# A hand-written order of work: the last batch's values in its own step, the second queries and the first placing later in layer 1, the last projection two ticks later

## What is computed

```python
x = rotate(x)                                   # layer 0 of the reference
for layer in (1, 2, 3):                         # "layer 0, 1, 2" of the kernel's loops
    h = modulate(layernorm(x))
    q, k, v = split(h @ w_qkv + b_qkv)          # 16 heads of 18
    if layer == 2:
        q, k = ln(q) * g + b, ln(k) * g + b     # per head: the kernel's "tok", "root", "inverse"
    o = softmax(q @ k.T * scale) @ v
    x = x + gate * (o @ w_proj + b_proj)
    x = x + gate2 * mlp(modulate(layernorm(x))) # layer 3: top 2 of 4 experts
```

## Time and profile before

| what | value |
|---|---|
| median of 3 runs | 1814.21 us (1813.95 to 1819.57) |
| the profiled execution's own time | 1822.59 us |
| its span in the profile | 1820.8 us |
| PE matmul busy | 1643.5 us, 90% of the span |
| DVE busy | 1227.4 us, 67% |
| ACT busy | 1055.5 us, 58% |
| POOL busy | 674.1 us, 37% |
| mean granted clock of PE | 0.947 of full speed |
| attention part of layers 0, 1, 2 (first to last exponential) | 213.3 to 479.2, 662.6 to 967.0, 1130.4 to 1388.4 us |

### The profile page before, as it was taken

How to read it: one execution, slowest core, us unless ns; L and a number is a source line. 1 busy time by engine, 2 the same in 40 slices (tenths; PEclk the granted TensorE clock), 3 DMA queues, 4 the chain that set the end, 5 groups by cost and what they waited for, 6 DMA issues and landing times.

```text
span 1820.8 us, 28323 instructions
## 1 busy us (share of the span) xinstructions
PE 1643.5 (90%) x9431; PEld 1068.6 (59%) x9431; DVE 1227.4 (67%) x2685; ACT 1055.5 (58%) x1897; POOL 674.1 (37%) x661
## 2 busy tenths in 40 slices
PE   5876899998899897999899999999988989999997
PEld 2433444443488663444336976444435878999997
DVE  7872677775265576767733656777763776888885
ACT  2322476756546346776674533767667556777773
POOL 4431222213356332433244533223233373343442
PEclk9996799998899888999989999999999999999999
DMA  7721333223000222232310021333322445566662
GB/s 245 245 92 43 94 109 106 90 89 89 28 4 1 81 68 90 70 98 68 118 50 21 1 92 50 103 107 90 95 87 73 123 137 165 162 169 174 171 172 46
DMA packets 106768, 178.16 MB, mean 98 GB/s; under 512 B 14331, under 2 KB 61107, under 8 KB 106335
## 3 DMA queue, kind: packets, MB, share of 16 engines
q1 hardware_dynamic: 100336, 167.07, 30.1%
q0 software_dynamic: 6288, 9.29, 2.7%
HBM read 124.73 MB, written 51.09 MB: 97 GB/s over the span
## 4 chain that ended last, share of the span: by engine, by line
PE 62%; DVE 11%; ACT 9%; DMA 6%; issue 5%; POOL 3%; SPq 3%; ACTq 0%; DVEq 0%; POOLq 0%
PE ps L2184 21%; PE ps L2269 12%; PE ps L2237 8%; PE ps L2223 7%; PE ps L2347 6%; PE ps L2205 4%; DMA heads_t<-stage 3%; ACT Pr L2018 3%; PE ps L2323 1%; DMA raw<-in_w 1%; DVE negmax L1412 1%; DVE GT L1338 1%; PE ps L2074 1%; ACT HQ L1993 1%; SPq L924 1%
## 5 line engine op out<-in xcount | busy, mean ns | idle before, releaser
L1412 DVE TENSOR_REDUCE negmax<-ps 128x1 f32<-128x512 f32 x768 | 488.1, 680 | 219.7 <-PE ps L2205 215.8
L2018 ACT ACTIVATE Pr<-ps 128x512 f32<-128x512 f32 x768 | 410.9, 602 | 212.1 <-PE ps L2223 211.9
L2223 PE MATMUL ps<-QK 55*128 55x512 f32 x768 | 238.4, 512 | 37.3 <-ACT Pr L2018 25.8
L2269 PE MATMUL ps<-W2a,G 128*128 128x288 f32 x1512 | 230.7, 300 | 9.6 <-DVE G L1775 5.7
L2269 PEld LDWEIGHTS ps<-W2a,G 128*128 128x128 f32 x1512 | 213.8, 190 | 21.4 <-DVE G L1775 13.1
L2237 PE MATMUL ps<-Pr,V 128*32 128x512 f32 x1536 | 220.4, 648 | 0.0
L2205 PE MATMUL ps<-QK 54*128 54x512 f32 x768 | 194.8, 439 | 21.2 <-DMA QK<-HQ 7.8
L2223 PEld LDWEIGHTS ps<-QK 55*128 55x128 f32 x768 | 91.9, 190 | 201.1 <-ACT Pr L2018 107.9
L2184 PE MATMUL ps<-HQ,W1a 128*128 128x512 f32 (+3 forms) x756 | 182.0, 381 | 7.3 <-ACT g L2034 5.9
L1775 DVE TENSOR_TENSOR G<-g,G 128x512 fp32r<-128x512 f32 (+1 forms) x201 | 152.4, 763 | 40.7 <-ACT G L2045 36.4
L1169 POOL TENSOR_TENSOR HQ<-act,HQ 128x512 fp32r<-128x512 f32 (+3 forms) x72 | 93.0, 1292 | 190.2 <-ACT HQ L1993 134.2
(11 more groups left out here) (294 smaller groups left out, 2670.2 us busy)
## 6 DMA issues: line engine op xcount, KB each, us to landing
QK<-heads_t SPq DMA_DIRECT2D x192, 144.0 KB
heads_t<-stage SPq DMA_DIRECT2D x96, 252.0 KB
raw<-in_w SPq DMA_DIRECT2D x34, 576.0 KB
raw<-in_w SPq DMA_DIRECT2D x38, 432.0 KB
QK<-heads_t SPq DMA_DIRECT2D x192, 72.0 KB
tok_rows<-blank SPq DMA_DIRECT2D x4, 2700.0 KB, 20.8
XG<-tok_rows SPq DMA_DIRECT2D x11, 540.0 KB, 4.8
WP<-in_w SPq DMA_DIRECT2D x39, 144.0 KB, 3.5
```

The source lines that it names most:

```text
L1412: dve.tensor_reduce(negmax[:, m % 2, h, t:t + 1], ps[:, row_bank(l, s, i), :], AX, ALU.max, negate=True).then_inc(a_free, 1)
L2018: act.activation(Pr[:, t % 2, 2 * half + pair, :], ps[:, (16 * s + u) % 3, :], ACT.Exp, scale=SCALE).then_inc(b_free, 1)
L2223: mm(ps[:, k % 3, :], QK[r:r + QROW + 1, g, 1, pair, 128 * t:128 * t + 128], QK[r:r + QROW + 1, g, 0, pair, :], start=True, stop=True).the ...
L2269: ins = mm(ps[:, t, 0:C], g_at(n)[:, x, 128 * t:128 * t + 128], W2[w_ % 2][:, w, ft, :], start=ft == 0 and p == 0, stop=ft == FT - 1 and p ...
```

## The change

Nothing is added to or taken from the work; only ticks change. In `attention_window`: for the last batch (window b = 2, y = 3) the four blocks of values go to ticks 25, 27, 28 and 30, in all layers; before they were at 1, 9, 17, 25 in layers 0 and 2, and at 4, 6, 15, 22 in layer 1. In layer 1, in every window, the first two projections go one tick later (10, 12 to 11, 13), the second block of queries one tick later (9 to 10), and the placing of group 0 from 11 to 13. In `leaving`, in all layers, the four projections of the last batch go from ticks 6, 8, 10, 12 of the dense part to 8, 10, 12, 14. The changed file's lines from 2000 on are 4 higher.

```diff
+VALUES = (25, 27, 28, 30)
...
-        turns = (10, 12, 18, 20) if l == 1 else (6, 10, 14, 18)
+        turns = (11, 13, 18, 20) if l == 1 else (6, 10, 14, 18)
...
-            out += [(t, "v", l, y, k) for k, t in enumerate((1, 9, 17, 25))]
+            out += [(t, "v", l, y, k) for k, t in enumerate((1, 9, 17, 25) if y < B - 1 else VALUES)]
...
-            out += [(t, "place", l, y, g) for g, t in enumerate((11, 16, 24, 32))]
+            out += [(t, "place", l, y, g) for g, t in enumerate((13, 16, 24, 32))]
...
-            out += [(t, "qk", l, y, j) for j, t in enumerate((7, 9, 14, 17, 27))]
-            out += [(t, "v", l, y, k) for k, t in enumerate((4, 6, 15, 22))]
+            out += [(t, "qk", l, y, j) for j, t in enumerate((7, 10, 14, 17, 27))]
+            out += [(t, "v", l, y, k) for k, t in enumerate((4, 6, 15, 22) if y < B - 1 else VALUES)]
...
-    out += [(6 + 2 * t, "proj", l, B - 1, t) for t in range(TT)] + [(15, "b2", l, 0, 0)]
+    out += [(8 + 2 * t, "proj", l, B - 1, t) for t in range(TT)] + [(15, "b2", l, 0, 0)]
```

## The result

| kernel | time | against the kernel before |
|---|---|---|
| before | 1814.1 us (4 runs) | |
| changed | 1839.6 us (4 runs, 1834.4 to 1846.7) | 1.0141, 95% interval 1.0112 to 1.0170 |
| changed, measured again | 1837.3 us (9 runs) | 1.0106, 1.0070 to 1.0141 |

The forecast was 1810.8 with a range to 1819.0. By the one comparison the change costs 25.6 us, by the other 19.3. The profiled execution of the changed kernel is its fastest in the first comparison (1834.4, span 1832.6), that of before is a long one for its kernel (1822.6), so the two traces differ by only 12 us. 4.7 us of what is missing lie in the opening, which has nothing of the change in it (208.6 us in after, 213.3 in before) and whose length differs from one execution to the next: 207.7 to 213.3 over the 18 traces of this study. So I compare lengths of steps, never absolute times.

What follows compares the result with a forecast made beforehand. The prediction took PE, busy 90% of the span, as the bound. Its terms, -6.0 + (0.75 + 1.7 + 1.15) - 3.5 + (1.8 + 1.8 - 1.1) = -3.4 us, took the median 1814.2 to 1810.8 us, range 1803.5 to 1819.0.

Steps and rivals of the forecast that it cites:

- What is moved out of such a step is gained: Layers 0 and 2, steps 8 to 10: chain stays on PE, so moved work is gained if it lands where PE waits.
- Part 1: Last batch's values, layers 0 and 2: three blocks leave steps 8 to 10, -3.0 us a layer, -6.0 in all.
- DVE or ACT sets 3.64: a block gives 1.0 us: Layers 0 and 2, steps 8 to 10: without its value block a pair of ticks falls from 4.64 to 3.64 us.
- rival A: Steps 12 and 13: filled gaps keep PE at 2.4 GHz, another -5.7 us, so 1805.1; chance 0.25.
- Rival C: Before step 12: maxima and load held by something like DRAM traffic, the -6.0 given back; +2.6, so 1816.8; chance 0.10.
- Part 2: Layer 1's second queries at tick 10, three windows: block leaves a stall's cover; +0.75, +1.7 and +1.15 us.
- Batch 2: Layer 1's third window: value block and its wait leave tick 15, but the placing's transfer has no slack; +1.15 us (0.5 to 1.9).
- Part 3: Last batch's values, layer 1: -2.0 from step 8, net -1.5 around the last query block and step 12; -3.5 us.
- 2.7 of clock: Layer 1, steps 12 and 13: of some 10 us at 1.2 GHz, 2.7 us come back if the gap no longer drops the clock.
- Part 4: Last projection, begin of the dense parts: +1.8 us each in layers 0 and 1, -1.1 in layer 2.
- in layer 2 the 1.98 us of waiting go: Begin of layer 2's dense part: PE's wait for oT vanishes, gates' product waits some 0.9 for DVE; -1.1 us.
- Rival B: Table loads and dense parts of layers 0 and 1: longer stalls lower the clock, +6.8 us in all, 1821.0; chance 0.10.

Runs made afterwards that it cites:

- h4: Kernel before with the last batch's second, third and fourth projection one tick earlier (6, 7, 9, 11) in layers 0 and 1: -1.5 us (-6.5 to +3.8).
- g4: Kernel before with, in layer 2 alone, the third and fourth block of the last projection two ticks later (6, 8, 12, 14): +3.1 us (-3.5 to +9.4).
- f4: Kernel before with only layer 1's first two projections at ticks 11 and 13 in place of 10 and 12: +5.4 us (0.4 to 10.5).
- g3: Kernel before with the last batch's values at 25, 27, 28, 30 in layers 0 and 2, at 15, 25, 28, 30 in layer 1: 0.0 us (-4.4 to +4.4).
- e4: Kernel before with only layer 1's second queries at tick 10, first two projections at 11 and 13, first placing at 13: +9.3 us (4.4 to 14.4).
- e1: Kernel before with only the last projection two ticks later in all three layers: +11.0 us (7.1 to 14.9).
- f1: The changed kernel itself, unaltered, measured again beside the kernel before: +19.3 us (12.7 to 25.6).
- h3: Changed kernel with the last projection as before, timed against the kernel before: +10.3 us (5.4 to 15.2).
- f3: Kernel before with the last projection two ticks later in layer 2 alone: +10.0 us (5.3 to 14.7).
- h2: Changed kernel with layer 1's second queries, projections and placing as before, timed against the kernel before: +14.9 us (8.9 to 20.9).
- e2: Kernel before with the last batch's values at ticks 25, 27, 28 and 30 in layers 0 and 2 alone: -0.7 us (-6.0 to +4.7).
- f2: Kernel before with the last projections two ticks later and layer 2's fourth weight load, third window, at tick 9 for 8: +15.1 us (7.8 to 22.3).
- g2: Kernel before with the last batch's values later in all layers and layer 2's fourth weight load, third window, at 10 for 8: +3.5 us (-2.4 to +9.4).

## Why the prediction was wrong, point by point

All 18 traces, sorted by whether the part is in. Means of a stretch's length in us, with the range; worked out from the starts of the exponentials that begin each step, a dense part from the start of the last one before it (h4 is left out of the first three rows, g4 of the fourth, f4 of the last; the row of layer 1's values leaves out g3 and every kernel with e4's or f4's lines).

```
stretch                          with the part            without                  difference
dense part, layer 0: leave        6: 186.2 (185.7-186.7)   11: 183.2 (182.4-184.0)   +3.0
dense part, layer 1: leave        6: 166.2 (165.9-167.4)   11: 164.6 (162.3-165.4)   +1.7
step 0, layer 2: leave in 0, 1    6:  18.3 (18.1-18.6)     11:  16.3 (14.9-19.8)     +2.0
dense part, layer 2: leave        6: 439.2 (436.6-442.9)   11: 434.0 (432.6-437.9)   +5.1
steps 8-15, layer 0: values       8: 131.2 (129.1-134.7)   10: 132.5 (128.6-138.1)   -1.2
steps 8-15, layer 2: values       8: 130.2 (128.1-134.1)   10: 130.2 (127.8-132.5)   -0.1
steps 8-15, layer 1: values       4: 142.2 (138.7-146.1)    8: 141.7 (139.0-144.4)   +0.5
steps 0-15, layer 1: queries      4: 309.5 (306.6-313.6)   13: 302.1 (298.4-308.1)   +7.4
```

The differences add to +18.4 us, beside +19.3 timed. The scatter of the traces allows some 6 us either way on that sum: the dense parts of layers 0 and 1 and layer 2's first step are certain to 1 us, the dense part of layer 2 to 2, and the rows of the steps to 2 to 4 each. The first four rows (+11.8) stand beside e1's +11.0, the last beside e4's +9.3. What no row has, the opening aside, takes 243.0 us in before, in after and in f1. So the result is placed in these rows, to that accuracy.

- **What bounds the kernel.** "What is moved out of such a step is gained" failed. The chain was on PE from score to score, but DVE was full in the same ticks, and ACT's exponentials held PE's scores too.
- **Part 1 (-6.0; found -1.3).** The failed step is the price of a block: "DVE or ACT sets 3.64: a block gives 1.0 us". The bare pair came from another layer's step without a half projection, and its length was taken as DVE's limit. In this pair DVE has six maxima, the transpose and the reciprocal, 4.5 us without a gap (rows of DVE above). The pair went from 4.64 to 4.66, the whole of steps 8 to 10 from 52.6 to 52.4. That is 0.2 us for three blocks, and the traces repeat to 0.1 us: even the lower bound, 0.6 a block, was too high. (The -1.2 of the table's longer stretch can't be told from 0.) That the blocks would fit into the 3.63 before step 12 was right (0.85 left); that SP's queue moves 3 us earlier was not, since nothing ahead of it had become shorter. Steps 12 to 15 are shorter by 0.2 and 0.3 in the mean, so rival A's prize for filling the gap did not come either. Rival C gave these -6.0 back as well, but by a queue held in DRAM; it was the gain that had never been there. The 2.6 us that the prediction quotes for a spill from the Trainium skill (page "DMA: Bandwidth & Descriptors", section "Anatomy of one DMA") is an estimate by a fit that the section gives for DMAs issued by POOL (GpSimd); this spill is SP's, took 5.14, and no term hangs on the 2.6.
- **Part 2 (+3.6; found +7.4).** Batch 0: forecast +0.75 (0 to 1.2), the traces -0.4, with up to 5 us between traces, so no more than small, as forecast: step 1 is 2.6 longer and step 2 2.7 shorter, for the placing's wait takes it back. Batch 1: forecast +1.7, the traces +1.4. Batch 2: forecast +1.15, steps 8 to 15 +6.7 (with 12 traces without it), and there the term fell. Step 9 is 3.6 longer in the three traces that have the last batch's values too than in the four with the values alone (24.4 against 20.8). The rest lies in steps 10 to 15, which differ by 3 us with the clock alone, whatever the edits (step 13: 18.2 us at 0.88 in before and in h3, 21.3 at 0.72 in after), so part of the 6.7, and of the 7.4, may be chance. Two things were missing in both windows that have a projection: that the first projection, now right behind the query block, waits for ACT to empty their bank (0.82 in step 5, 0.52 in step 9), and the clock, which in step 9 goes from 0.85 to 0.78. And where the value block left tick 15 its wait of 1.01 went, as the forecast had it, but another came in its place, for the exponentials (step 9 of after):

```profile
858.60 0.40 PE L2227 MATMUL ps<-QK 55*128 55x512 f32 x1
860.26 0.79 PE L2227 MATMUL ps<-QK 55*128 55x512 f32 x1 [1.26 <-ACT Pr L2022]
```

  The transfer that the forecast took for the bound of batch 2 shows no wait in after: PE comes too late for it to be one.
- **Part 3 (-3.5; found +0.5).** The wait behind the last query block was right to 0.05 us, and step 12's wait took most of it, as forecast. Steps 8 to 11 became 4.5 us longer and 12 to 15 were 4.0 shorter, where the forecast had 6.5 (3.8 of wait and 2.7 of clock). What failed are the -2.0 in step 8 (it gave 0.5: 18.9 for 19.4) and the 2.7 of clock "given back".
- **Part 4 (+2.5; found +11.8).** The mechanism in layers 0 and 1 was right, waits and block (+1.8 each; +3.0 and +1.7). The failed step is "in layer 2 the 1.98 us of waiting go": the forecast never asked what is late next. It was POOL's shift and what follows it, in whose shadow the wait lay. -1.1 became +4.5 at tile 8: 2.2 for the block, 1.7 for the wait of the gates' product, which the forecast had seen and priced at 0.9, and 1.4 for half clock after the 3.10 us wait (3.25 for the seven matmuls at 1413.09, 1.89 for the same seven at full speed), less the 0.8 by which that wait ends earlier. Of the 4.5 some is won back further on: f1 and f3, without the late scatter, are 2.8 and 3.1 late at tile 28, but h2 5.6. The 2.0 in layer 2's first step (granted clock 0.63 in 8 us of it, below) neither the forecast nor a rival had named.
- **Rival B** had the sign and, with +6.8, a third of the size. Its clock is part of it, not most: over the nine runs of f1 the mean granted clock is 0.952, over the 29 of before beside them 0.954, by which the changed kernel spends 0.002 x 2 x 1830 = some 7 us more at 1.2 GHz, worth at most 4 of its 19 us. The Trainium skill ("TensorE: Matmul & The Clock Gate", section "HAM oscillation") makes bursts with idling between them the thing to avoid; here the trace agrees for the stalls that were made longer (0.78 for 0.85 in e4's step 9), while the gaps that were filled gave nothing measurable back.

Stretch of 8 us from the begin of layer 2, after, then before:

```profile
1134.60:1142.60 8.00, 7.66 (x29) 3.94 (x29) 4.23 (x7) 3.52 (x7) 4.82 (x2) 0.63 0.55 167
```

```profile
1130.40:1138.40 8.00, 7.29 (x39) 3.65 (x39) 5.05 (x9) 4.59 (x9) 4.80 (x2) 1.00 0.59 169
```

29 matmuls in place of 39, with next to no wait. All six traces with the leave in layer 1 take 18.1 or more for the step; of the other twelve four take 16.9 or more, and three of these 18.1 or more. Why the clock falls there I can't say, and that the leave makes it fall rests on these counts.

## What to carry to other kernels

A block on the chain costs its own length only if no other engine is full in the same ticks: add up the other engines' records between the same two marks, in that very place, before you price its removal. And a wait that you mean to take away has a shadow: find what the next dependent instruction waits for, and what else stands in that shadow for nothing. Work that fills a wait is not to be moved past it (e1). Whether moving it towards the wait's start pays, one trace suggests (h4, 0.9 to 2.5 us in layer 0) and no timed run shows.

## What was not expected of the hardware

- In these traces the landing of small scatters goes with who goes first. In the eleven traces where SP issued the 432 KB load after the last scatter's issue had ended, POOL waited 1.68 or 1.69 us; in the seven where the load was issued before that (after, e1, e2, f2, f4, g2, h3) it waited 3.31 to 4.01, and PE lost 4.5 to 7 us between tiles 24 and 28 against before; the eleven lost nothing there. The net price is smaller: the seven had won 1.5 to 3.9 us between tiles 8 and 21, the eleven at most 1.7, and at tile 28 they are some 3 us behind traces with the same place of the projection. The changed kernel shows both: 3.31 in the first trace, 1.69 in f1's. Two kernels meant to change the order did not move it, so this rests on the 18 traces, not on an edit. POOL of f1:

```profile
1511.37 1.26 POOL L1235 DMA_INDIRECT tok_rows<-XG,idx  x1 [0.30 <-issue]
1514.31 2.93 POOL L1252 TENSOR_TENSOR tmp<-euler,tmp 128x16 f32<-128x16 f32 x1 [1.69 <-DMA tok_rows<-XG,idx]
```

- The same kernel varies by 20 us from run to run (before: 1805 to 1843 over all calls), and its traces differ most where the clock does. The changed kernel's two, after and f1: layer 1's attention 313.6 and 306.8 us, layer 2's steps 8 to 15 128.1 and 131.0, but the dense parts of layers 0 and 1 agree to 0.2 us.
